# A gated cross-attention and mixture-of-experts block on one core: first tokens loaded by row tile, the first batch's work shared between engines, instruction lists written anew

## The chip, the core and the metric

The kernel runs on one core of a Trainium2 chip. The core has a matrix engine (TensorE, PE in the rows; its weight loads are PEld), VectorE (DVE), ScalarE (ACT), GpSimd (POOL), and SyncE (SP), which here only issues DMAs. Each engine runs its own list of instructions strictly in order and waits on semaphores; nothing is reordered while the kernel runs. The metric is the device time of one execution, in microseconds (us).

## What is computed

```python
# x (4,512,512); fside = weights (4,512,512); ctx = weights (4,512,256)
def smooth_quant_linear(x, w):            # x [T,D], w [O,D]
    s  = sqrt(max(amax(|x|,0),EPS) / max(amax(|w|,0),EPS))
    xs, ws = x / s, w * s
    x_scale = max(amax(|xs|,-1),EPS)/127;  w_scale = max(amax(|ws|,-1),EPS)/127
    return round(xs/x_scale) @ round(ws/w_scale).T * x_scale * w_scale.T
def layer1(x, guw, dw):                   # for each of the 4 batches
    gate, up = split(smooth_quant_linear(x, guw))
    return smooth_quant_linear(silu(gate) * up, dw)
def layer2(t):                            # 2048 tokens, width 512
    top-2 of 16 experts by softmax(t @ gate_w.T); each expert takes its first 256 tokens
    expert(t) = (silu(t @ w_gate) * (t @ w_up)) @ w_down        # inner width 352
    shared(t) = (silu(t @ ws_gate) * (t @ ws_up)) @ ws_down     # inner width 704
x = x + tanh(g_xattn) * layer1(layernorm(x), fside, ctx)
x = x + tanh(g_ffn)   * layer2(layernorm(x))
```

All of it is in float32. The matmuls of layer 2 split each operand into a rounded high part and the rest and add three products (high*high, high*low, low*high); they are the helper `three`, lines 1854 to 1856.

## The kernel before

Tokens lie as 4 batches of 512, each batch as 4 row tiles j of 128 partitions; x2 holds them throughout. A batch's layer 1 is a long chain that crosses all engines ("a" is its first product, "b" its second). The steps of a batch, by their names in the code:

- `stats_a` (DVE: bn_stats and bn_aggr of the four tiles), `norm_a` (POOL: a power gives 1/sqrt), `normalise_a` (ACT, L635: writes xn).
- The column peaks. For batch 0: `turn_w`, `turn_x` (PE transposes of weights w1 and of xn) and `amax_w`, `amax_x` (DVE, L1102). For later batches: `abs_w`, `abs_x` (ACT), `peaks_*` (DVE, L1107) and a short transpose.
- `ratio_a`, `root_a` (POOL), `smooth_a`; `row_rs`, `row_s` (PE) spread the factors over partitions; `scale_x`, `x_steps` (DVE), `copy_s` (ACT), `scale_w` (POOL, L486), `w_steps` (DVE, L1222).
- `quant_x`, `quant_w` (ACT, L642: rounding by adding a large constant), `turn_qx`, `turn_qw` (PE), `ints_x`, `ints_w` (ACT), `product_a` (PE, L1969), `dequant_a` (DVE, L1285), `silu_a` (ACT, L713), `gate_up` (DVE, L1299).
- The same for "b" with weights w2, ending in `add_x` (DVE, L1315), `stats_b`, `norm_b`, `normalise_b` (ACT, L754: writes y), `turn_y`, `x_hi` (ACT), `x_lo` (DVE), `logits` and the top-two choice. `store_x2n` writes y to DRAM. `positions`, `slot_rows`, `table`, `add_table`, `index` turn the choices of all four batches into the token list of each expert.

Beside it, POOL and ACT split the shared expert's weights: `split_gu_hi` (ACT), `split_gu_lo` (POOL, L502, four pieces), `split_d_*`. The first `shared_up` waits for all four pieces. The shared expert (`shared_up`, `shared_down` by batch, half and 128-wide chunk) fills PE between the steps of batches 1 to 3. Where nothing can fill, `keep_busy(n)` (L1896) writes n matmuls to an unused bank. Five of the eight token halves are done so; the three of `TAIL` are left for the end, where their shared expert runs as two more "experts" of inner width 352, while the routed rows are gathered back.

After that come the 16 experts. A step of expert e: `up` (its 352 inner columns as two chunks of 128 and a chunk of 96, whose gate and up parts are packed into one bank), `hidden` (ACT silu, L992; DVE product, L1715; ACT high part, L996; DVE low part, L1717), `down` with the sum over chunks, and `turn_tokens` for e+1. ACT's `weights_gu` (L793 to L796) and `weights_d` (L802) make the high parts of the next expert's weights, DVE's (L1446, L1459) the low parts. For a chunk m of the last unit ACT must also copy the packed up part (L990, L991) and DVE adds it (L1712).

What sets the order: for PE, DVE, ACT and POOL a list of calls written out by hand, up to the loop over experts; for SP the order of the `dma_start` calls. Expert 0's gate and up weights are loaded by themselves; expert 1's four transfers (gate 704 KB, up 704 KB, down 512 and 192 KB) go out together when `sh_gu` says that the last shared_up is done, and ACT's first `weights_gu(1, 0, 1)`, which stands ahead of `hidden(0, ...)` on ACT, waits for all four.

At the end DVE adds the gathered rows into x2 (`add_rows` by half batch, `add_last` by tile of batch 3, L1789 and L1792), and `last_rows` (L1783) adds the last unit's result, after which SP stores the tile.

## Time and profile before

| | us |
|---|---|
| median of 3 runs (579.65, 580.83, 579.65) | 579.65 |
| the profiled execution | 581.87 |
| its span, first to last instruction | 579.8 |
| PE busy in the span | 546.2 (94%) |
| DVE, ACT, POOL busy | 419.4, 331.0, 154.3 |
| mean granted clock of TensorE | 0.985 |

```profile
PE   7897879999999999999799999999999999999995
...
DVE  3778988998899786586376666766676776566766
...
PEclk9988999999999999999899999999999999999998
DMA  7930130014001130115757776666777767457742
```

These are busy tenths in 40 slices of 14.5 us. PE's line says nothing of use: the fillers of `keep_busy` count as busy. They all lie in the first 92 us. The granted clock falls in slices 3 and 4, in slice 20 (275 to 290 us) and in the last.

### The profile page before, as it was taken

Reading aid. Unit: us, or ns where it says so; the run is one execution under the profiler, and the core shown is the slowest. Engines: PE = TensorE matmul, PEld = TensorE weight load, DVE = VectorE, ACT = ScalarE, POOL = GpSimd, SP = SyncE. Lnnn points to the kernel's source line nnn. Section 1 sums busy time; section 2 is a strip of 40 time slices with the busy share of each in tenths; the row PEclk is TensorE's granted clock in tenths of the full one; section 3 lists DMA queues with packets and bytes.
Section 4 is the critical chain, followed back from the end, with each engine's and each line's share of the span. In section 5 each row is a group of like instructions: output and inputs, shape, how many; then the busy total and the mean of one; then the engine's idle time right before and its main releaser. Section 6 shows DMA issues by size and latency. Waiting matters only on the chain.

```text
span 579.8 us, 10175 instructions
## 1 busy us (share of the span) xinstructions
PE 546.2 (94%) x3768; PEld 464.0 (80%) x3776; DVE 419.4 (72%) x828; ACT 331.0 (57%) x570; POOL 154.3 (27%) x187
## 2 busy tenths in 40 slices
PE   7897879999999999999799999999999999999995
PEld 3453548986888788887799999999999999999983
DVE  3778988998899786586376666766676776566766
ACT  3285876686558527522367677766666666742321
POOL 3437780431043010104022211111111100166610
PEclk9988999999999999999899999999999999999998
DMA  7930130014001130115757776666777767457742
GB/s 265 386 131 2 37 136 11 2 37 145 1 5 35 73 101 1 77 46 165 244 165 263 246 252 222 222 222 227 242 244 260 245 218 241 148 167 214 232 147 99
DMA packets 45891, 89.52 MB, mean 154 GB/s; under 512 B 4304, under 2 KB 24784, under 8 KB 44832
## 3 DMA queue, kind: packets, MB, share of 16 engines
q1 hardware_dynamic: 40736, 72.26, 36.7%
q0 software_dynamic: 5120, 16.78, 9.3%
q8 instruction: 23, 0.38, 0.3%
q14 instruction: 12, 0.10, 0.0%
HBM read 72.25 MB, written 16.78 MB: 154 GB/s over the span
## 4 chain that ended last, share of the span: by engine, by line
PE 62%; DVE 19%; ACT 6%; POOL 6%; issue 4%; DMA 2%; another core or an unknown queue 1%; SPq 0%; DVEq 0%; POOLq 0%; ACTq 0%
PE ps_gu L1854 10%; PE ps_gu L1855 10%; PE ps_gu L1856 10%; PE ps_d L1854 6%; PE ps_d L1856 5%; PE ps_d L1855 5%; PE ps_a L2108 3%; PE ps_gu L1896 2%; POOL w L486 2%; DMA raw_d<-in_L_ffn_w_down 2%; PE ps_gu L2415 2%; POOL sw_lo L502 1%; PE ps_d L1875 1%; DVE bn_b L1093 1%; ACT y L754 1%
## 5 line engine op out<-in xcount | busy, mean ns | idle before, releaser
L1854 PE MATMUL ps_gu<-ex_xhi,w_hi 128*128 128x256 f32 x352 | 99.4, 283 | 0.2 <-DVE ex_xlo L1469 0.2
L1855 PE MATMUL ps_gu<-ex_xlo,w_hi 128*128 128x256 f32 x352 | 99.5, 283 | 0.0
L1856 PE MATMUL ps_gu<-ex_xhi,w_lo 128*128 128x256 f32 x352 | 99.4, 282 | 0.0
L1854 PEld LDWEIGHTS ps_gu<-ex_xhi,w_hi 128*128 128x128 f32 x352 | 67.0, 190 | 2.5 <-DVE ex_xlo L1469 0.5
L1855 PEld LDWEIGHTS ps_gu<-ex_xlo,w_hi 128*128 128x128 f32 x352 | 67.1, 191 | 1.8
L1856 PEld LDWEIGHTS ps_gu<-ex_xhi,w_lo 128*128 128x128 f32 x352 | 67.1, 191 | 0.0
L1854 PE MATMUL ps_gu<-xt_hi,sw_hi 128*128 128x256 f32 x220 | 65.1, 296 | 0.1
L996 ACT ACTIVATE ex_hhi<-ex_hid 128x256 fp32r<-128x256 f32 (+1 forms) x66 | 27.5, 417 | 64.6 <-DVE ex_hid L1715 58.0
L1855 PE MATMUL ps_gu<-xt_lo,sw_hi 128*128 128x256 f32 x220 | 62.0, 282 | 0.0
L1856 PE MATMUL ps_gu<-xt_hi,sw_lo 128*128 128x256 f32 x220 | 62.0, 282 | 0.0
L1854 PE MATMUL ps_d<-wd_hi,ex_hhi 128*128 128x512 f32 x132 | 54.3, 411 | 6.6 <-DVE ex_hlo L1717 6.5
L1717 DVE TENSOR_TENSOR ex_hlo<-ex_hid,ex_hhi 128x256 fp32r<-128x256 f32 (+1 forms) x66 | 28.0, 424 | 33.8 <-ACT ex_hhi L996 30.9
L1856 PE MATMUL ps_d<-wd_hi,ex_hlo 128*128 128x512 f32 x132 | 52.1, 395 | 0.0
L1855 PE MATMUL ps_d<-wd_lo,ex_hhi 128*128 128x512 f32 x132 | 51.9, 393 | 0.0
L586 POOL DMA_INDIRECT got<-expert_out_scratch,slot_col x32 | 33.1, 1036 | 67.4 <-DMA expert_out_scratch<-eo 51.6
L549 POOL COPY idx_col<-idx 128x2 uint32 (+1 forms) x16 | 5.5, 342 | 157.5 <-PE ps_a L2108 132.7
L1896 PE MATMUL ps_gu<-ident_b 128*128 128x512 bf16 x158 | 43.5, 414 | 3.6 <-POOL fold L446 3.6
L1854 PEld LDWEIGHTS ps_gu<-xt_hi,sw_hi 128*128 128x128 f32 x220 | 41.7, 190 | 3.2 <-issue 0.7
L1446 DVE TENSOR_TENSOR w_lo<-raw_gu,w_hi 128x1024 fp32r<-128x1024 f32 x36 | 43.8, 1218 | 0.0
L1855 PEld LDWEIGHTS ps_gu<-xt_lo,sw_hi 128*128 128x128 f32 x220 | 41.8, 190 | 1.0
L1856 PEld LDWEIGHTS ps_gu<-xt_hi,sw_lo 128*128 128x128 f32 x220 | 41.8, 190 | 0.0
L1715 DVE TENSOR_TENSOR ex_hid<-ex_silu,ps_gu 128x256 f32<-128x256 f32 x44 | 18.3, 416 | 32.2 <-ACT ex_silu L992 31.6
(255 smaller groups left out, 1411.4 us busy)
## 6 DMA issues: line engine op xcount, KB each, us to landing
raw_gu<-in_L_ffn_w_gate SPq DMA_DIRECT2D x16, 704.0 KB
raw_gu<-in_L_ffn_w_up SPq DMA_DIRECT2D x16, 704.0 KB
raw_d<-in_L_ffn_w_down SPq DMA_DIRECT2D x16, 512.0 KB
expert_out_scratch<-eo SPq DMA_DIRECT2D x16, 512.0 KB
w<-in_fside_BxS2xS SPq DMA_DIRECT2D x4, 1024.0 KB, 5.4
x2n_scratch<-y SPq DMA_DIRECT2D x4, 1024.0 KB, 3.9
x<-in_x SPq DMA_DIRECT2D x1, 3072.0 KB, 16.5
raw_d<-in_L_ffn_w_down SPq DMA_DIRECT2D x16, 192.0 KB
```

The source lines that it names most:

```text
L486: last = pool.tensor_tensor(w1[:, j, :], w1[:, j, :], line_a[:], ALU.mult)
L586: pool.indirect_dma_start(got[k][:, j, n, :], None, eo_dram, bass.IndirectOffsetOnAxis(slot_col[:, b, j, n:n + 1], 0)).then_inc(got_in[b][ ...
L996: act.activation(ex_hhi[0:k, m, :], ex_hid[0:k, (q + m) % 2, :], ACT.Copy).then_inc(ex_hi, 1)
L1446: dve.tensor_tensor(w_lo[q][:, g], raw_gu[q][:, g, :, 0:OWN], w_hi[q][:, g].bitcast(F32), ALU.subtract)
L1715: dve.tensor_tensor(ex_hid[0:k, (q + m) % 2, :], ex_silu[0:k, (q + m) % 2, :], up, ALU.mult).then_inc(ex_h, 1)
L1717: dve.tensor_tensor(ex_hlo[0:k, m, :], ex_hid[0:k, (q + m) % 2, :], ex_hhi[0:k, m, :].bitcast(F32), ALU.subtract).then_inc(ex_lo, 1)
L1854: pe.matmul(dst, a_hi, b_hi, start=start, stop=False)
L1855: pe.matmul(dst, a_hi, b_lo, start=False, stop=False)
L1856: return pe.matmul(dst, a_lo, b_hi, start=False, stop=stop)
L1896: pe.matmul(ps_gu[:, 1, :], ident_b[:], ident_b[:].unsqueeze(1).broadcast_to((P, J, P)), start=True, stop=True)
L2108: last = pe.transpose(ps_xt[:, c, h * P:(h + 1) * P], xg[q][:, h, c * P:(c + 1) * P], ident[:])
L2415: last = pe.matmul(folded, wb[q][:, c, :], ex_xhi[xq][:, c, :], start=(c == 0), stop=(c == C - 1))
```

## The change

Computed values stay the same. It has seven parts:

1. SP loads batch 0's tokens in four DMAs, one for each row tile, ahead of w1; `stats_a(0)` waits for each tile by itself.
2. For batch 0, `normalise_a` moves from ACT to DVE (between the second and third `amax_w`), half of `quant_w` moves to DVE (`quant_w_rest`), and `silu_a` and `gate_up` run as two halves. `normalise_b(0)` moves from ACT to DVE.
3. The lists of PE, ACT, DVE and POOL are written anew, from the first instruction to the first expert. The first `keep_busy` goes from 23 to 13. `stats_a(3)` moves from batch 0's `stats_b` to behind batch 1's. On DVE `w_steps(1)` goes ahead of `dequant_b(0, ...)`. On POOL `split_gu_lo(2)` goes behind the first `norm_b`.
4. Expert 1's down weights are loaded after its gate and up weights have landed, and `weights_gu(1)` waits for these alone.
5. `store_x2n(2)` goes behind the load of expert 0's gate and up weights; DVE's `weights_d(0, 0)` goes behind `tokens(0, 0)`.
6. In the very last unit the packed chunk is computed second instead of third (`part_at`).
7. At the end DVE's `add_last` steps all stand ahead of the last `hidden`, and `last_rows` adds the first half as soon as its own matmuls are done.

(The last two new functions in it, `normalise_a` and `quant_w_rest`, are DVE's; `normalise_b` on DVE is like the former, from x2 to y.)

```diff
+    def part_at(e, m):
+        return (0, 2, 1)[m] if e == NE - 1 else m
...
-            sp.dma_start(x2[:, 0], x_v[0]).then_inc(x0_in, 16)
+            for j in range(J):
+                sp.dma_start(x2[:, 0, j, :], x_v[0][:, j, :]).then_inc(x0_in[j], 16)
...
-            store_x2n(2)
             sp.wait_ge(gated_done, B)
             load_gu(0, wg_v[0], wu_v[0])
+            store_x2n(2)
             store_x2n(3)
...
-            load_raw(1, 1)
+            load_gu(1, wg_v[1], wu_v[1])
+            sp.wait_ge(raw_in[1], 32)
+            load_d(1, w_down[1])
...
+            def quant_w_first(a):
+                act.wait_ge(w_steps_done[LA], a + 1)
+                for j in range(HALF):
+                    last = act.activation(w1[:, j, :], w1[:, j, :], ACT.Copy, bias=MAGIC + LOW16, scale=small[LA]["w_inv"][:, j:j + 1])
+                last.then_inc(qw_done[LA], 1)
...
+            def silu_half(a, h):
+                t = slice(HALF * h, HALF * h + HALF)
+                for j in range(HALF * h, HALF * h + HALF):
+                    emptied_a(act, unit_a(a, A_H + j))
+                act.activation(gated[:, t, :], xn[:, t, 0:I2], ACT.Silu).then_inc(silu_done if h else silu_first_done, 1)
...
-                act.wait_ge(raw_in[q], 32 if isinstance(e, int) and e == 0 else 64 * k + 64)
+                act.wait_ge(raw_in[q], 32 if isinstance(e, int) and e < 2 else 64 * k + 64)
...
+            def normalise_a(a):
+                dve.wait_ge(rstd_a_done, 4 * a + 4)
+                for j in range(J):
+                    last = dve.tensor_scalar(xn[:, j, :], x2[:, a, j, :], rstd_a[:, a, j:j + 1], shift_a[:, a, j:j + 1], ALU.mult, ALU.add)
+                last.then_inc(xn_done, 1)
+            def quant_w_rest(a):
+                dve.wait_ge(w_steps_done[LA], a + 1)
+                for j in range(HALF, J):
+                    last = dve.tensor_scalar(w1[:, j, :], w1[:, j, :], small[LA]["w_inv"][:, j:j + 1], MAGIC + LOW16, ALU.mult, ALU.add)
+                last.then_inc(qw_rest_done, 1)
...
-                dve.wait_ge(ex_d, M * NE)
                 dve.wait_ge(sum_last, HALF)
                 for k in range(HALF):
                     j = HALF * h + k
+                    if k == 0:
+                        dve.wait_ge(first_half_done, 1)
+                    else:
+                        dve.wait_ge(ex_d, M * NE)
...
-            keep_busy(23)
+            keep_busy(13)
             turn_w(0, 0)
...
             turn_w(0, 3)
-            turn_w2(0, 0)
+            keep_busy(5)
             turn_x(0, 0)
...
-            hidden(E + 5, 1, 1)
-            add_last(1)
+            add_last(3)
             hidden(E + 5, 1, 2)
-            add_last(2)
-            add_last(3)
             last_rows()
```

The order on VectorE at the start: bn_a is the statistics, amax_w_a and amax_x_a the column peaks of weights and tokens, xn the normalised tokens. Before:

```order
L1084 BN_AGGR mv_a<-bn_a 128x2 x4
L1102 TENSOR_REDUCE amax_w_a<-ps_a 128x1 x4
L1102 TENSOR_REDUCE amax_x_a<-ps_a 128x1 x4
L1176 SCALAR_TENSOR_TENSOR recip_w_a<-amax_w_a,ones 128x4
L1183 RECIPROCAL recip_w_a<-recip_w_a 128x4
```

Now:

```order
L1110 BN_AGGR mv_a<-bn_a 128x2 x4
L1128 TENSOR_REDUCE amax_w_a<-ps_a 128x1 x2
L1326 TENSOR_SCALAR xn<-x_49,rstd_a,shift_a 128x512 x4
L1128 TENSOR_REDUCE amax_w_a<-ps_a 128x1 x2
L1128 TENSOR_REDUCE amax_x_a<-ps_a 128x1 x4
L1202 SCALAR_TENSOR_TENSOR recip_w_a<-amax_w_a,ones 128x4
```

Four passes over 512 elements have moved in among the eight reductions.

VectorE between batch 1's quantisation and the end of batch 0's layer 1: w_max_a is `w_steps(1)`, y<-ps_d is `dequant_b(0)`, x_49<-x_49,y is `add_x(0)`, bn_b and bn_a are `stats_b(0)` and `stats_a(3)`. Before:

```order
L1230 RECIPROCAL x_inv_a<-x_step_a 128x4
L1285 SCALAR_TENSOR_TENSOR y<-ps_d,x_step_b,line_b 128x512 x4
L1222 TENSOR_REDUCE w_max_a<-w_118 128x4
L1176 SCALAR_TENSOR_TENSOR w_step_a<-w_max_a,consts 128x4
L1230 RECIPROCAL w_inv_a<-w_step_a 128x4
L1315 TENSOR_TENSOR x_49<-x_49,y 128x2048
L1061 MEMSET consts 128x1
L1093 BN_STATS bn_b<-x_49 128x6 x4
L1061 MEMSET consts 128x1
L1097 BN_AGGR mv_b<-bn_b 128x2 x4
L1061 MEMSET consts 128x1
L1079 BN_STATS bn_a<-x_49 128x6 x4
```

Now:

```order
L1256 RECIPROCAL x_inv_a<-x_step_a 128x4
L1248 TENSOR_REDUCE w_max_a<-w_118 128x4
L1202 SCALAR_TENSOR_TENSOR w_step_a<-w_max_a,consts 128x4
L1256 RECIPROCAL w_inv_a<-w_step_a 128x4
L1311 SCALAR_TENSOR_TENSOR y<-ps_d,x_step_b,line_b 128x512 x4
L1370 TENSOR_TENSOR x_49<-x_49,y 128x2048
L1085 MEMSET consts 128x1
L1119 BN_STATS bn_b<-x_49 128x6 x4
L1085 MEMSET consts 128x1
L1123 BN_AGGR mv_b<-bn_b 128x2 x4
L1311 SCALAR_TENSOR_TENSOR xn<-ps_a,x_step_a,line_a 128x512
```

`w_steps(1)` has moved ahead of `dequant_b(0)`, and `stats_a(3)` is gone from here.

VectorE at the very end: got is a gathered row tile, the last row is `last_rows`. Before:

```order
L1712 TENSOR_TENSOR ex_up<-ex_up,ps_gu 64x256
L1715 TENSOR_TENSOR ex_hid<-ex_silu,ex_up 96x256
L1717 TENSOR_TENSOR ex_hlo<-ex_hid,ex_hhi 96x256
L1789 SCALAR_TENSOR_TENSOR x_49<-got_179,wts,x_49 128x512
L1792 SCALAR_TENSOR_TENSOR x_49<-got_179,wts,x_49 128x512
L1789 SCALAR_TENSOR_TENSOR x_49<-got_179,wts,x_49 128x512
L1792 SCALAR_TENSOR_TENSOR x_49<-got_179,wts,x_49 128x512
L1783 SCALAR_TENSOR_TENSOR x_49<-ps_d,tg,x_49 128x512 x2
```

Now:

```order
L1772 TENSOR_TENSOR ex_up<-ex_up,ps_gu 64x256
L1775 TENSOR_TENSOR ex_hid<-ex_silu,ex_up 96x256
L1777 TENSOR_TENSOR ex_hlo<-ex_hid,ex_hhi 96x256
L1852 SCALAR_TENSOR_TENSOR x_49<-got_179,wts,x_49 128x512
L1855 SCALAR_TENSOR_TENSOR x_49<-got_179,wts,x_49 128x512
L1775 TENSOR_TENSOR ex_hid<-ex_silu,ps_gu 128x256
L1777 TENSOR_TENSOR ex_hlo<-ex_hid,ex_hhi 128x256
L1846 SCALAR_TENSOR_TENSOR x_49<-ps_d,tg,x_49 128x512 x2
```

The last chunk is a plain one, and no gathered row stands between its low part and the last two additions.

## Rows read from the trace of the kernel before

**Rows 1.** the stages of the span (columns in the first line)
```profile
core 0: us, PE busy (x) PEld busy (x) DVE busy (x) ACT busy (x) POOL busy (x), PEclk, DMA share, GB/s
0.00:92.20 92.20, 75.85 (x423) 42.54 (x427) 67.77 (x126) 56.06 (x73) 50.30 (x71) 0.94 0.42 152
92.20:272.00 179.80, 174.91 (x1303) 149.84 (x1307) 149.21 (x359) 101.02 (x182) 36.02 (x41) 1.00 0.14 48
272.00:300.00 28.00, 24.08 (x156) 21.53 (x154) 14.18 (x26) 13.81 (x24) 5.10 (x6) 0.94 0.65 207
300.00:540.00 240.00, 239.89 (x1682) 221.80 (x1681) 162.19 (x276) 150.82 (x271) 53.70 (x61) 1.00 0.70 229
...
556.75:579.80 23.05, 15.83 (x98) 13.67 (x98) 16.41 (x28) 4.23 (x11) 0.00 (x0) 0.92 0.24 92
```

**Rows 2.** the page's costliest groups: filler matmuls, and the halving of the hidden values
```profile
L1896 PE MATMUL ps_gu<-ident_b 128*128 128x512 bf16 x158 | 43.5, 414 | 3.6 <-POOL fold L446 3.6
...
L1717 DVE TENSOR_TENSOR ex_hlo<-ex_hid,ex_hhi 128x256 fp32r<-128x256 f32 (+1 forms) x66 | 28.0, 424 | 33.8 <-ACT ex_hhi L996 30.9
```

**Rows 3.** timeline of the first 19 us (start us, us, engine line op)
```profile
3.62 8.03 PE L1896 MATMUL ps_gu<-ident_b 128*128 128x512 bf16 x23 [3.62 <-POOL fold L446]
...
10.51 2.93 ACT L635 ACTIVATE xn<-x,shift_a,rstd_a 128x512 f32<-128x512 f32 x4 [3.57 <-POOL shift_a L456]
...
12.12 1.34 DVE L1102 TENSOR_REDUCE amax_w_a<-ps_a 128x1 f32<-128x512 f32 x2 [3.62 <-PE ps_a L1875]
...
18.13 0.16 DVE L1176 SCALAR_TENSOR_TENSOR recip_w_a<-amax_w_a,ones 128x4 f32<-128x4 f32 x1
```

**Rows 4.** the issue of the first batch's weights at 1.25 (KB, us to landing)
```profile
w<-in_fside_BxS2xS SPq DMA_DIRECT2D x1, 1024.0 KB, 7.7
```

**Rows 5.** timeline, 30 to 46 us
```profile
30.95 2.56 ACT L642 ACTIVATE w<-w,w_inv_a 128x512 f32<-128x512 f32 x4
...
42.67 1.06 ACT L713 ACTIVATE gated<-xn 128x1024 f32<-128x1024 f32 x1 [0.40 <-DVE xn L1285]
...
45.01 5.04 POOL L502 TENSOR_TENSOR sw_lo<-raw_sgu,sw_hi 128x352 fp32r<-128x352 f32 x4
...
45.04 0.66 PE L1875 MATMUL ps_d<-ident,gated 128*128 128x128 f32 x4 [0.69 <-DVE gated L1299]
```

**Rows 6.** timeline, 65 to 86 us
```profile
65.41 4.99 POOL L486 TENSOR_TENSOR w<-w,line_a 128x512 f32<-128x512 f32 x4 [3.12 <-ACT line_a L677]
...
73.13 3.11 DVE L1315 TENSOR_TENSOR x<-x,y 128x2048 f32<-128x2048 f32 x1
...
81.13 2.93 ACT L754 ACTIVATE y<-x,shift_b,rstd_b 128x512 f32<-128x512 f32 x4 [1.84 <-POOL shift_b L456]
...
82.28 3.60 POOL L502 TENSOR_TENSOR sw_lo<-raw_sgu,sw_hi 128x352 fp32r<-128x352 f32 x4
```

**Rows 7.** groups of VectorE by line and shape (busy us, mean ns)
```profile
L1390 DVE TENSOR_SCALAR pos_oh<-slot_no,r_pos 128x256 bf16<-128x256 bf16 x32 | 6.6, 281 | 0.1
...
L1107 DVE TENSOR_TENSOR abs_b<-abs_b 128x512 f32<-128x512 f32 x6 | 4.1, 679 | 0.0
```

**Rows 8.** timeline around the first expert, 268 to 295 us
```profile
268.74 0.37 SPq L325 DMA_DIRECT2D raw_gu<-in_L_ffn_w_gate  x1
...
279.97 1.91 ACT L793 ACTIVATE w_hi<-raw_gu 128x2048 fp32r<-128x2048 f32 x1 [6.57 <-DMA raw_d<-in_L_ffn_w_down]
...
284.48 0.50 PE L1854 MATMUL ps_d<-wd_hi,ex_hhi 128*128 128x512 f32 x1 [3.70 <-DVE ex_hlo L1717]
...
294.89 1.90 ACT L793 ACTIVATE w_hi<-raw_gu 128x2048 fp32r<-128x2048 f32 x1
```

**Rows 9.** timeline of the end
```profile
572.43 0.74 DVE L1789 SCALAR_TENSOR_TENSOR x<-got,wts,x 128x512 f32<-128x512 f32 x1
...
572.56 0.50 PE L1854 MATMUL ps_d<-wd_hi,ex_hhi 96*128 96x512 f32 x1 [1.65 <-DVE ex_hlo L1717]
...
575.51 1.41 DVE L1783 SCALAR_TENSOR_TENSOR x<-ps_d,tg,x 128x512 f32<-128x512 f32 x2
```

More of the change, by code:

```diff
@@ L980, in _, with hidden @@
             shared_hi(2, 1, 5)
+            weights_d(0, 0)
             tokens(0, 0)
-            def hidden(e, q, m, first):
-                n, k = M * e + m, ROWS[m]
+            def hidden(e, q, m, first, part=None):
+                part = m if part is None else part
+                n, k = M * e + m, ROWS[part]
                 if first and m == 0:
@@ L1473, in _ @@
             amax_w(0, 1)
+            normalise_a(0)
             amax_w(0, 2)
@@ L1509, in _ @@
             x_steps(1)
+            w_steps(1)
             dequant_b(0, 0)
@@ L1513, in _ @@
             dequant_b(0, 3)
-            w_steps(1)
             add_x(0)
             stats_b(0)
-            stats_a(3)
             dequant_a(1, 0)
+            normalise_b(0)
             dequant_a(1, 1)
@@ L1670, in _ @@
             shared_lo(1, 1, 3)
+            count(2)
             shared_lo(1, 1, 4)
@@ L2426, in fill_d @@
                                  wd_hi[q][0:k, m, :], wd_lo[q][0:k, m, :], first, final)
+                    if halves is not None and h == 0:
+                        last.then_inc(halves, 1)
                 last.then_inc(ex_d, 1)
```

515 lines of the change are left out of this document (270 added, 245 removed).

## The prediction, as put down before the changed kernel had run

> **What bounds the kernel now.** I read the span by stages first [rows 1]. From 92.2 to 272 us, where the shared expert fills PE, PE is busy 174.91 of 179.8 us, and from 300 to 540, in the expert loop, 239.89 of 240. There only less matmul work would help, and the change takes none away. So the gain must come from three other places. Up to 92.2 us PE is busy 75.85 us, but 43.5 us of the filler matmuls [rows 2] all lie there: the useful part is about 32 us, and the stage is a chain through DVE (67.77 us busy), ACT and POOL. From 272 to 300 PE has 24.08 of 28 us. After 556.75 it has 15.83 of 23.05. The timeline of each place then shows which wait ends last.
>
> **The start, to the first batch's gated values.** PE runs 23 fillers up to 11.65 (8.03 us, 0.35 each), turns the weights, and DVE's eight reductions begin at 12.12 and end before 18.13 [rows 3]. The weights, issued at 1.25, are there 7.7 us later, at 8.95 [rows 4]: PE comes to them 2.7 us late. With 13 fillers it is there at 3.62 + 13 x 0.35 = 8.2, so the weights decide. They are issued some 1.4 us later now, behind four token DMAs instead of one, but behind the same bytes: 9.0 to 10.3, I take 9.4. Reductions then start at 9.4 + 0.47 = 9.9, 2.2 us earlier. Against this DVE has four new passes of 128x512 between them. No row shows such a pass: the nearest are a TENSOR_SCALAR over 256 bf16 elements with 0.28 us and a float32 pass over 512 elements with 0.68 [rows 7]. Each is off in one respect, so I take the middle, 0.45: 1.8 us (1.1 to 2.7). The gap between reductions pays 0.3 back. Net 2.2 - 1.8 + 0.3 = **0.7 us** earlier (-1.1 to 1.8). The row-tile load itself earns nothing here: ACT began `normalise_a` at 10.51 [rows 3] because POOL was done then, and DVE in the new list gets there at about 11.3.
>
> The Trainium skill, page "VectorE: DVE Perf Modes", section on the perf-mode tiers, has 1227 ns for a float32 tensor_scalar of 2048 elements in SBUF, some 0.3 to 0.4 us for a quarter as an estimate; with it this step would earn about 1.1 instead of 0.7.
>
> `quant_w(0)` takes ACT 2.56 us [rows 5], with ACT as the engine that all wait for; half of it on DVE beside ACT saves **1.3**. Silu takes 1.06 us after the last dequantisation [rows 5], and the product 1.2 behind it; in halves the first silu runs under the last two dequantisations and the second under the first product: **1.1**. Tokens' peaks start 3.1 us earlier, at 41.9 in place of 45.04 [rows 5].
>
> **From there to the first shared_up.** Batch 1's `scale_w` is five us of POOL, 65.41 to 70.4, and `w_steps(1)` waits for it; `add_x(0)` stands behind and begins at 73.13 [rows 6]. In the new list `scale_g` stands behind batch 1's `ratio_a`, so POOL takes the root, and ACT copies the factors, while DVE has work. Walking DVE's list with the durations of before, I get `w_steps(1)` at about 62 and the end of `stats_b(0)` at about 74.6 in place of 79.1: 1.4 more. `normalise_b(0)` takes ACT 2.93 us [rows 6]; on DVE 1.8 by the price above: 1.1 more. `stats_a(3)` (some 2.8 us, four passes of 0.68 and small ones) no longer delays `dequant_a(1)`, which the turn of y waits for on PE: 0.5. Together 3.1 + 1.4 + 1.1 + 0.5 = **6.1 us** at the first shared_up: 86.1 in place of 92.2. POOL must have split all four pieces by then: `norm_b(0)` ends at 76.5, then 1.3 + 3.6 + 3.6 [rows 6] gives 85.0. It just fits.
>
> One thing speaks against it. A split of the same size took 3.60 us at one place and 5.04 at another, beside DVE's work [rows 5, 6], and `add_x(0)` took 3.11 beside POOL [rows 6]. The Trainium skill, "SBUF — State Buffer", section "Who interferes with whom", has a rule for this: DVE's tensor_scalar from SBUF to SBUF, in its two-port modes, excludes GpSimd, "Whoever issues first gets the shared pair for the whole instruction". Both moved normalisations and `quant_w_rest` are such instructions, and the trace of before has none beside POOL. If each split takes 5.04 in place of 3.60, POOL is done at 85.0 + 2.9 = 87.9, and this part earns 4.3 instead of 6.1.
>
> **92 to 272 us.** PE's own work is the same; its 4.9 us of idle time may change. DVE is 149.21 of 179.8 us busy and now owes `stats_a(3)`. I take **1 us back** (between 4 back and 1.5 more gained): PE's fillers give room, but batch 3's chain must keep pace.
>
> **Expert 0 and 1.** Expert 1's weights go out at 268.74; ACT starts on them at 279.97, behind the last of four transfers, and PE waits 3.70 us, to 284.48, for `hidden(0, 0)`, which stands behind them on ACT [rows 8]. Now ACT waits for 1408 of 2112 KB. Of the 11.2 us, some 2 pass before data flow; two thirds of the rest is 6.1: 276.8, **3.2 us** earlier (0 if the gathers beside it slow it as much). The wait shrinks to 0.5. The clock comes with it: 0.94 over 28 us [rows 1] means 3.4 us at 1.2 instead of 2.4 GHz, 1.7 us of lost work; without the long wait I count **1.4** of that. The new SP wait holds back the down weights and then expert 2's load: 279.96 becomes some 281.2. ACT needs these at 294.89 [rows 8] less 4.6, 290.3, and that load takes about 8 us: it fits with 1 us. Sum **4.6** (0.5 to 5.2).
>
> `weights_d(0, 0)` behind `tokens(0, 0)` on DVE, and `store_x2n(2)` behind a load, cost nothing: both end before what waits for them, the first under PE's 5.7 us of up. If that cover goes, each costs up to 2 us.
>
> **The end.** The last chunk's low part is ready at 572.5 and PE waits 1.65 us for it [rows 9]. A plain chunk needs no copies of the packed part (two) and no addition, 0.4 us each; what is left is four steps of 0.42 [rows 2]: ready at 571.3, **1.2 us** earlier. Then DVE adds two tiles, four passes from 572.43, and only then the last rows, 575.51 to 576.92 [rows 9]. PE's first half ends 1.2 us after its start, so now: 572.5, and two additions to 574.0. That is 2.9 us earlier in all; DVE's third gathered tile may end just behind the silu, so I take **2.6** (1.2 to 3.6).
>
> **The sum.** 6.1 - 1.0 + 4.6 + 2.6 = 12.3 us. The profiled execution goes from 581.87 to 569.6 and its span from 579.8 to 567.5; the median of the runs lies 2.2 us below the profiled one, and from 579.65 I get **567.4**.
>
> **The rivals.**
> - The front's gain is given back where DVE sets the pace. For: 83% busy, and waits of PE there of 1 us and less show batch chains just in time. Against: DVE has 30 us idle there. Left are 4.6 + 2.6: 572.4.
> - POOL's splits decide, by the exclusion above: 569.2.
> - The change does not do what it says: the gate and up weights share their time with the gathers and land hardly earlier, and PE waits at expert 0 as before: 12.3 - 4.1, 571.5.
> - Slower: the token list. `index()` needs batch 3's top two, and PE's `turn_tokens(0, 0)` needs the gathers behind `index()`. If batch 3 is late by the new DVE list, PE has no fill left and waits; each us late is a us of time, plus half of what runs at the low clock. It decides from the point where batch 3's chain is 7.2 us later than now, as all that experts and end earn is then gone; a delay of 10 gives 582.5. Against it: PE reaches that place without waiting today, and the new list keeps the same steps between the last `table` and `turn_tokens`.
>
> **Chances.** As forecast 0.50; DVE's pace 0.27; POOL 0.10; weights land late 0.07; slower by the token list 0.06. A measurement can tell about 0.2% (1.2 us) from no change. The first four are all faster by more, less 0.03 for the pace rival at its worst together with a bad end: faster 0.91, same 0.03, slower 0.06. The range takes in the bounds: best 7.5 + 1.5 + 5.2 + 3.6 = 17.8 gives 561.9, worst of the faster cases 3 - 4 + 3.5 + 1.7 = 4.2 gives 575.5. The tail beyond both is under 0.2.
>
> **What would show it.** The first shared_up at 86 us (a later start with PE fillers before it: the front failed; POOL's last sw_lo ending there: the port). The new TENSOR_SCALAR lines at 0.28 to 0.68 us each. PE's idle time from shared_up to `turn_tokens(0, 0)` under 7 us. ACT's first w_hi of expert 1 some 8 us after its load's issue, PE's longest wait there under 1 us and no slice with a low clock. PE's last wait under 0.6 us and the last x addition directly behind the last matmul. The forecast is wrong if the stage from 86 to 265 grows by more than its share, or if the weights' load is slowed by the gathers.

## The result, and the profile after

The changed kernel takes 583.31 us (median of 7 runs, 582.73 to 585.32) against 579.65 (578.91 to 580.83, 7 runs) for the one before: ratio 1.0067, 95% interval 1.0052 to 1.0082. It is slower, by 3.7 us in the median, where I had said 12 faster. Its profiled execution took 582.95 us, with a span of 580.9; PE is busy 540.6 us of it, DVE 431.6, ACT 325.2, POOL 152.0, at a mean clock of 0.985. The experiments ran later, on four chips (the kernel before beside each), where in many executions the end of every kernel is slower, the kernel before among them (579.3 to 597.3 us on the last of them), so that each ratio compares only those runs of a kernel that lie within 1.5% of its fastest. Besides the ratios I compare landmarks of the traces; those of "before" and "changed" come from the first measurement.

Four of them cut the span: the first shared_up on PE, POOL's copy of the first token list (`idx_col`), POOL's copy for the last expert, and POOL's first gather of result rows. From the third to the fourth it is 55.2 to 55.4 us in all traces. Of the changed kernel they read (timeline: start us, us, engine line op):

```profile
100.17 0.28 PE L1917 MATMUL ps_gu<-xt_hi,sw_hi 128*128 128x256 f32 x1
...
271.75 0.22 POOL L558 COPY idx_col<-idx 128x2 uint32<-128x2 uint32 x1 [25.55 <-DVE idx L1463]
...
454.13 0.31 POOL L558 COPY idx_col<-idx 128x2 uint32<-128x2 uint32 x1 [9.91 <-PE ps_a L2173]
...
509.46 0.97 POOL L595 DMA_INDIRECT got<-expert_out_scratch,slot_col  x1 [51.61 <-DMA expert_out_scratch<-eo]
```

The kernel before has 92.36, 262.83, 449.45 and 504.73 there, and ends at 579.8 instead of 580.9. The difference by stretch:

| stretch | before | changed | difference | predicted |
|---|---|---|---|---|
| start to first shared_up | 92.36 | 100.17 | +7.8 | -6.1 |
| to the first token list | 170.47 | 171.58 | +1.1 | +1.0 |
| to the last expert's tokens | 186.62 | 182.38 | -4.2 | -4.6 |
| to the first result rows | 55.28 | 55.33 | 0 | 0 |
| from there to the end | 75.07 | 71.44 | -3.6 | -2.6 |

Three of the four terms came out within a microsecond. The whole miss is in the first stretch, which alone is 13.9 us off. Its end in the windows of the changed kernel (columns in the first line), to be held against the first line of [rows 1]:

```profile
core 0: us, PE busy (x) PEld busy (x) DVE busy (x) ACT busy (x) POOL busy (x), PEclk, DMA share, GB/s
0.00:92.20 92.20, 63.35 (x369) 36.31 (x373) 72.54 (x118) 44.62 (x58) 46.85 (x71) 0.92 0.41 140
...
272.00:300.00 28.00, 26.89 (x170) 22.88 (x170) 18.84 (x32) 13.56 (x25) 10.07 (x11) 1.00 0.72 231
...
55.00:60.00 5.00, 3.04 (x14) 2.28 (x13) 4.83 (x10) 0.76 (x2) 4.49 (x6) 0.78 0.01 2
60.00:65.00 5.00, 4.84 (x35) 3.65 (x34) 4.90 (x5) 4.27 (x10) 2.76 (x4) 0.88 0.01 2
70.00:75.00 5.00, 3.72 (x16) 1.95 (x17) 3.97 (x7) 4.12 (x6) 5.00 (x5) 0.66 0.00 0
...
80.00:85.00 5.00, 2.37 (x11) 0.70 (x8) 3.79 (x7) 2.82 (x3) 4.38 (x7) 1.00 0.45 171
85.00:90.00 5.00, 0.00 (x0) 0.00 (x0) 5.00 (x2) 0.00 (x0) 5.00 (x7) 0.51 0.00 0
90.00:95.00 5.00, 3.05 (x12) 2.18 (x13) 3.91 (x6) 1.19 (x2) 0.70 (x1) 0.50 0.47 193
```

From 85 to 90 us PE and ACT do nothing at all, DVE has two instructions and POOL seven; and when PE resumes, it is at half its clock until about 95. Its clock is also low from 55 to 65 and from 70 to 75 us, which will matter below. The timeline of the changed kernel has the instruction that all wait for:

```profile
82.19 1.26 POOL L522 TENSOR_TENSOR sd_lo<-raw_sd,sd_hi 64x512 fp32r<-64x512 f32 x1
...
82.28 9.62 DVE L1333 TENSOR_SCALAR y<-x,rstd_b,shift_b 128x512 f32<-128x512 f32 x4 [0.95 <-POOL shift_b L465]
...
83.42 7.28 POOL L511 TENSOR_TENSOR sw_lo<-raw_sgu,sw_hi 128x352 fp32r<-128x352 f32 x8
...
91.95 1.12 PE L1938 MATMUL ps_d<-ident,y 128*128 128x128 f32 x4 [9.54 <-DVE y L1333]
```

That is `normalise_b(0)`: four passes priced at 1.8 us that took 9.62. The answer for that line alone shows how they share it, one long and three short:

```profile
L1333 DVE TENSOR_SCALAR y<-x,rstd_b,shift_b x4: 534/840/7644, 82.3 to 91.4; 128x512 f32<-128x512 f32 x4
```

The nanoseconds are shortest, median and longest. The long one is the first, from 82.28 to 89.92; POOL's row of splits, one behind the other, ends at 90.70, and the last of them starts at 89.6. POOL's eight took 0.91 us each in the mean, as long as before ([rows 6]: four in 3.60).

The start lost a little too. The statistics begin sooner than the single load allowed, but the fourth tile comes late, and so do the weights:

```profile
4.44 0.69 DVE L1105 BATCH_NORM_STATS2 bn_a<-x 128x6 f32<-128x512 f32 x1 [2.00 <-DMA x<-in_x]
...
7.78 0.69 DVE L1105 BATCH_NORM_STATS2 bn_a<-x 128x6 f32<-128x512 f32 x1 [1.00 <-DMA x<-in_x]
...
10.46 0.66 PE L1938 MATMUL ps_a<-ident,w 128*128 128x128 f32 x4 [2.42 <-DMA w<-in_fside_BxS2xS]
...
12.42 1.91 DVE L1326 TENSOR_SCALAR xn<-x,rstd_a,shift_a 128x512 f32<-128x512 f32 x4
...
18.73 0.17 DVE L1202 SCALAR_TENSOR_TENSOR recip_w_a<-amax_w_a,ones 128x4 f32<-128x4 f32 x1
...
40.08 4.05 POOL L511 TENSOR_TENSOR sw_lo<-raw_sgu,sw_hi 128x352 fp32r<-128x352 f32 x4 [2.92 <-ACT sw_hi L627]
...
41.93 2.76 DVE L1347 TENSOR_TENSOR gated<-gated,xn 128x512 f32<-128x512 f32 x2
```

`recip_w_a`, the end of the eight reductions, stands at 18.73 against 18.13 [rows 3], and the two half products of gate and up take 2.76 us, beside a split of POOL. Experts and end did as foreseen; of the timeline and of SP's issues:

```profile
276.89 0.38 SPq L331 DMA_DIRECT2D raw_gu<-in_L_ffn_w_gate  x1
...
285.04 1.91 ACT L816 ACTIVATE w_hi<-raw_gu 128x2048 fp32r<-128x2048 f32 x1 [3.21 <-DMA raw_gu<-in_L_ffn_w_up]
...
575.40 0.50 PE L1917 MATMUL ps_d<-wd_hi,ex_hhi 128*128 128x512 f32 x1 [0.44 <-DVE ex_hlo L1777]
...
576.48 1.41 DVE L1846 SCALAR_TENSOR_TENSOR x<-ps_d,tg,x 128x512 f32<-128x512 f32 x2 [1.13 <-PE ps_d L1919]
```

ACT has its weights 8.15 us after their issue (11.2 before, [rows 8]), PE's longest wait there is 0.5 us instead of 3.70, and the last wait is 0.44 instead of 1.65 [rows 9].

### The profile page after: what moved, and what is told of

It reads as the page before. It is cut to its first block, busy times and chain, and to the rows that moved or that the text cites. A ratio compares the mean times of both kernels' runs of the same rounds, so it can differ in the third digit from the quotient of the medians.

```text
span 580.9 us, 10139 instructions
## 1 busy us (share of the span) xinstructions
PE 540.6 (93%) x3748; PEld 460.7 (79%) x3756; DVE 431.6 (74%) x839; ACT 325.2 (56%) x561; POOL 152.0 (26%) x187
## 4 chain that ended last, share of the span: by engine, by line
PE 63%; DVE 18%; ACT 4%; DMA 3%; issue 3%; POOL 1%; SPq 0%; DVEq 0%; ACTq 0%
PE ps_gu L1917 10%; PE ps_gu L1918 10%; PE ps_gu L1919 10%; PE ps_d L1917 6%; PE ps_d L1919 5%; PE ps_d L1918 5%; PE ps_a L2173 3%; DMA raw_d<-in_L_ffn_w_down 2%; DVE y L1333 2%; PE ps_a L2034 2%; PE ps_gu L2483 1%; PE ps_d L1938 1%; DMA raw_gu<-in_L_ffn_w_up 1%; PE ps_a L1953 1%; PE ps_gu L2485 1%
## 5 line engine op out<-in xcount | busy, mean ns | idle before, releaser
L1917 PE MATMUL ps_d<-wd_hi,ex_hhi 128*128 128x512 f32 (+1 forms) x132 | 54.4, 412 | 1.5 <-DVE ex_hlo L1777 1.2
L595 POOL DMA_INDIRECT got<-expert_out_scratch,slot_col x32 | 34.6, 1082 | 68.7 <-DMA expert_out_scratch<-eo 51.6
L1919 PE MATMUL ps_d<-wd_hi,ex_hlo 128*128 128x512 f32 (+1 forms) x132 | 52.1, 394 | 0.0
L1918 PE MATMUL ps_d<-wd_lo,ex_hhi 128*128 128x512 f32 (+1 forms) x132 | 51.9, 393 | 0.0
L1918 PEld LDWEIGHTS ps_gu<-xt_lo,sw_hi 128*128 128x128 f32 x220 | 41.9, 190 | 0.8
L1959 PE MATMUL ps_gu<-ident_b 128*128 128x512 bf16 x138 | 37.6, 400 | 3.6 <-POOL fold L455 3.6
L562 POOL DMA_INDIRECT xg<-x2n_scratch,idx_col x32 | 34.1, 1065 | 17.6 <-POOL idx_col L558 12.7
```

The lines of the kernel that those rows point to most:

```text
L562: pool.indirect_dma_start(xg[q][:, h, :], None, x2n_dram, bass.IndirectOffsetOnAxis(idx_col[:, q, h:h + 1], 0)).then_inc(xg_in[q], 16)
L595: pool.indirect_dma_start(got[k][:, j, n, :], None, eo_dram, bass.IndirectOffsetOnAxis(slot_col[:, b, j, n:n + 1], 0)).then_inc(got_in[b][ ...
L1917: pe.matmul(dst, a_hi, b_hi, start=start, stop=False)
L1918: pe.matmul(dst, a_hi, b_lo, start=False, stop=False)
L1919: return pe.matmul(dst, a_lo, b_hi, start=False, stop=stop)
L1959: pe.matmul(ps_gu[:, 1, :], ident_b[:], ident_b[:].unsqueeze(1).broadcast_to((P, J, P)), start=True, stop=True)
```

## The experiments

The landmarks of the traces in us, with the stretches behind them. Names are those of the runs below.

| kernel | first shared_up | to token list | to last expert | result rows to end |
|---|---|---|---|---|
| before | 92.36 | 170.5 | 186.6 | 75.1 |
| changed | 100.17 | 171.6 | 182.4 | 71.4 |
| e1, e8: changed, normalise_b(0) on ACT | 92.28, 94.30 | 172.6, 172.7 | 181.8, 182.4 | 81.3, 85.2 |
| e2: changed, POOL waits | 92.25 | 172.1 | 182.3 | 89.9 |
| e3: before, normalise_b(0) on DVE | 95.96 | 170.6 | 187.4 | 83.6 |
| e4: before, down weights last | 89.56 | 170.6 | 182.6 | 83.5 |
| e5: before, new end | 91.61 | 170.6 | 188.2 | 73.0 |
| e7, e12: before, both | 91.58, 90.37 | 170.6, 170.6 | 182.7, 182.6 | 71.3, 72.0 |
| e6: e1 and one load | 91.92 | 172.8 | 182.2 | 79.6 |
| e9: changed, other form | 100.72 | 171.6 | 182.2 | 89.8 |
| e10: e6, held split, fillers | 88.75 | 172.8 | 182.9 | 82.1 |
| e11: e7, one gather ahead | 90.28 | 170.6 | 182.5 | 102.2 |
| e13: changed again | 101.63 | 171.6 | 182.4 | 84.4 |
| e14, e15, e16: e10, ACT's stream shifted | 89.84, 89.08, 89.65 | 172.8, 172.8, 172.8 | 183.2, 182.7, 181.9 | 89.7, 83.6, 84.2 |

My theory after the result: DVE's passes over SBUF stand still as long as POOL's instructions follow each other without a gap. The rivals: the form of pass is slow by itself, or the front is late for other reasons and the pass only fills a wait.

**Put the step back, or clear the way for it.** e1 takes `normalise_b(0)` out of DVE's list and puts it into ACT's:

```diff
@@ ACT's list
             split_gu_hi(3)
+            normalise_b(0)
             x_hi(0, 0)
@@ DVE's list
             dequant_a(1, 0)
-            normalise_b(0)
```

> The changed kernel with one step put back: normalise_b(0) runs on ACT again, behind its last split, instead of on DVE. Theory A (DVE's pass is starved by GpSimd's splits of the shared weights): ACT writes y in about 2.9 us from 82.3 on, so y is there at 85.2 instead of 91.9; GpSimd's four pieces end near 90.7 as now and set the first shared_up at about 92.5 instead of 100.7. Time 575.5 us (573 to 577.5), from 583.3. Rival B (the front is late for other reasons, the new list above all, and the pass only fills a wait): first shared_up stays at 99 or later, time 582 to 583.5.

e2 leaves it on DVE and makes POOL wait for it:

```diff
             norm_b(0)
+            pool.wait_ge(x2n_done, 1)
             split_d_lo(1)
```

> The changed kernel with one wait more: GpSimd starts its last three splits (the small down piece and gate-up pieces 2 and 3) only when normalise_b(0) on DVE is done. Theory A (starvation by GpSimd): each of DVE's four passes of 128x512 takes 0.45 to 0.6 us, y is there at 84.3; GpSimd's 8.6 us of splits then end near 93, the first shared_up is at about 93.5, time 576 us (574 to 579). Rival B (this form of pass is slow by itself, whoever is beside it): the passes still take 9.6 us in sum, GpSimd ends at 100.5, time 583 to 585.

In both the first shared_up moved to where the theory had it or sooner: 92.28 (92.5 expected) and 92.25 (93.5). Not all of the 7.9 us against the changed kernel's 100.17 is the pass, though. `shift_b`, from which y can start, already stands at 82.04 in the changed kernel and at 80.03 and 81.06 in these two; PE's clock was low between 55 and 75 us in the changed kernel's trace (0.78, 0.88, 0.66), and 1.00 there in both of these. From the start of `shift_b` to the first shared_up the changed kernel takes 18.1 us (18.1 again in e13), e1 12.3 and e2 11.2: the pass and the low clock behind it cost 5.9 to 6.9 us. The 2.0 us before it, against e1, are PE's slow steps: it spreads `rsmooth_a` in 2.04 us from 57.74 where e1 takes 1.16, and all that waits for it is late. In e2's timeline the same four passes at the same place take 1.91 us, with POOL idle behind them:

```profile
81.29 1.91 DVE L1334 TENSOR_SCALAR y<-x,rstd_b,shift_b 128x512 f32<-128x512 f32 x4 [0.58 <-POOL shift_b L465]
...
83.28 1.27 POOL L522 TENSOR_TENSOR sd_lo<-raw_sd,sd_hi 64x512 fp32r<-64x512 f32 x1 [2.03 <-DVE y L1334]
...
84.52 7.63 POOL L511 TENSOR_TENSOR sw_lo<-raw_sgu,sw_hi 128x352 fp32r<-128x352 f32 x8
...
87.98 3.39 DVE L1134 TENSOR_TENSOR abs_b<-abs_b 128x512 f32<-128x512 f32 x1
```

So form and data are not slow, POOL's row of splits is what the passes wait for. The last line shows it on another form: a pass that takes 0.68 us elsewhere [rows 7] took 3.39, until POOL was nearly through. Times: e1 has ratio 1.0124 (1.0057 to 1.0190), e2 1.0089 (1.0029 to 1.0149). The 575.5 and 576 us that I expected were not seen, though the first result rows are gathered at 502.07 and 501.92, earlier than in the kernel before (504.73): both traces lose it after that, in 81.3 and 89.9 us instead of 71.4. e8 is e1 once more:

> The same kernel as in the first of these experiments (normalise_b(0) back on ACT, all else as changed), since there the part after 505 us was disturbed. Up to the first gather of result rows it stood at 502.07 us, where the kernel before stood at 504.73 and the changed one at 509.46. Theory (starvation was the whole loss of the front, and the rest of the front is neutral): 575.5 us, ratio 0.993, 1.3% under the changed kernel. Rival (something else of the new lists costs time later): 579 or more.

It gave 580.81 us at best and a ratio of 1.0069 (1.0018 to 1.0120); its trace stands at 504.68 at the first result rows and then takes 85.2 us. By time the rival came out (579 or more): the loss comes in the last stretch, whose cause is taken up below.

**One part alone in the kernel before.** e3:

```diff
@@ ACT's list
-            normalise_b(0)
@@ DVE's list
             dequant_a(1, 0)
+            normalise_b(0)
             dequant_a(1, 1)
```

> The kernel before with one part of the change alone: normalise_b(0) on DVE, behind dequant_a(1, 0), and not on ACT. Theory A (starvation): GpSimd's splits run there too, from about 81 to 89, so y is complete only near 89 instead of 84, the first shared_up moves from 92.4 to about 97, time 583 to 588 us against 579.65. Rival B (the prediction's price, 0.45 us a pass): y 1.1 us earlier, time 578.5 to 579.7.

```profile
82.99 3.76 POOL L502 TENSOR_TENSOR sw_lo<-raw_sgu,sw_hi 128x352 fp32r<-128x352 f32 x4
...
83.25 4.70 DVE L1299 TENSOR_SCALAR y<-x,rstd_b,shift_b 128x512 f32<-128x512 f32 x4
...
88.00 1.12 PE L1882 MATMUL ps_d<-ident,y 128*128 128x128 f32 x4 [3.58 <-DVE y L1299]
```

Here POOL has only four splits in a row, and the passes take 4.70 us. y is there at 88.0 (I said 89), the first shared_up at 95.96 (97), ratio 1.0123 (1.0075 to 1.0172). The wait follows the length of POOL's row: 3.5 us of it are left when DVE begins, and 2.8 us are lost over e2's 1.91; in the changed kernel 8.4 are left and 7.7 lost. In the old lists `split_gu_lo(2)` was done long before; the new lists put it directly behind `split_d_lo(1)`, so the row is twice as long.

**Another form of the same step.** e9:

```diff
-                    last = dve.tensor_scalar(y[:, j, :], x2[:, b, j, :], rstd_b[:, j:j + 1], shift_b[:, j:j + 1], ALU.mult, ALU.add)
+                    last = dve.scalar_tensor_tensor(out=y[:, j, :], in0=x2[:, b, j, :], scalar=rstd_b[:, j:j + 1],
+                                                    in1=shift_b[:, j:j + 1].broadcast_to((P, D)), op0=ALU.mult, op1=ALU.add)
```

> The changed kernel with normalise_b(0) still on DVE, at the same place in its list, but as four scalar_tensor_tensor instructions (in1 is the shift, one value per row, spread over the row) instead of four tensor_scalar. The trace of the changed kernel has scalar_tensor_tensor passes beside GpSimd's work at 0.70 to 0.75 us each. Theory (only some forms of a DVE instruction are kept waiting by GpSimd, tensor_scalar among them): four passes in 2.8 to 3.2 us, y at 85.3 in place of 91.9, first shared_up at 92 to 93 in place of 100.2. Rival (any DVE pass from SBUF to SBUF waits while GpSimd's instructions follow each other): 8 us or more again, first shared_up at 100.

```profile
81.55 10.64 DVE L1333 SCALAR_TENSOR_TENSOR y<-x,rstd_b,shift_b 128x512 f32<-128x512 f32 x4
...
82.55 7.10 POOL L511 TENSOR_TENSOR sw_lo<-raw_sgu,sw_hi 128x352 fp32r<-128x352 f32 x8
```

My theory of forms fell, the rival is right: 10.64 us, the first pass alone 8.65, first shared_up at 100.72, ratio 1.0286 (1.0183 to 1.0388). The scalar_tensor_tensor passes that run undisturbed beside POOL, the dequantisations, read their product from PSUM. So the name of the instruction does not decide, and where its inputs lie seems to. Nor is every read of SBUF held up: the kernel before computes the statistics of x, in SBUF, from 76.28 to 78.75 us beside POOL's down splits (74.04 to 78.62) in 0.69 and 1.86 us (one pass, then three), as long as in the changed kernel with POOL idle. Which property of a pass decides, no run here isolates.

**The load by row tile.** e6 is e1 with one DMA for the first tokens, and the waits on it to match:

```diff
-            for j in range(J):
-                sp.dma_start(x2[:, 0, j, :], x_v[0][:, j, :]).then_inc(x0_in[j], 16)
+            sp.dma_start(x2[:, 0], x_v[0]).then_inc(x0_in, 16)
...
```

> As the one before, and the first tokens loaded by one DMA again instead of four by row tile. Theory (four issues ahead of the weights and a late fourth tile delay statistics and the first transposes): the first statistics end near 8.1 us instead of 8.5 to 9.7, PE's first transposes start near 9.5 instead of 10.5 to 11.5, and the time falls by 1 to 1.5 us against that kernel, to 574.3. Rival (the pieces cost nothing): the same time within 0.3 us.

The first statistics end at 8.2, PE turns the weights from 9.00 (10.46 in the changed kernel and 10.47 in e1), and `recip_w_a` stands at 17.26 instead of 18.73: 1.5 us for four issues ahead of the weights. The weights are issued at 2.65 us behind four issues and at 1.25 behind one, and land 7.8 and 7.7 us later: the later issue counts in full. In the six traces with four loads `recip_w_a` stands at 18.73 to 20.21, in the five of the same lists with one load (e6, e10, e14 to e16) at 16.91 to 17.57. The gain lives as far as `shift_b` (78.55 instead of e1's 80.03), but the first shared_up is only 0.4 earlier, at 91.92: PE waits 3.3 us for y, and its granted clock is 0.65 and 0.67 from 80 to 90 us. The time was 575.77 us at best and 587.28 in the median of six runs, which gives no ratio with an interval; the expected 574.3 was not reached.

**Both repairs of the rest.** e10 is e6 with two edits more: it holds POOL's first split until the gated values are done, and gives PE eight fillers ahead of the first transpose of y:

```diff
@@ POOL's list
             norm_a(1)
+            pool.wait_ge(gated_done, 1)
             split_gu_lo(0)
@@ PE's list
+            keep_busy(8)
             turn_y(0, 0)
```

> The kernel with normalise_b(0) on ACT and one load of the first tokens, and two edits more: GpSimd starts its first split only when the first batch's gated values are done, and PE has eight fillers more ahead of turn_y(0, 0). Theory for the first edit (the two half products of gate and up, 2.76 us, waited for that split): they take 1.3 us, and the first transposes of the gated values start at 41.8 instead of 43.3. Theory for the second (PE idle before turn_y lets the clock fall): no 5 us slice under 1.00 from 80 to 92, and from shift_b to the first shared_up 10.0 to 11.2 us instead of 13.4. First shared_up at 87.5 to 90 instead of 91.9. Rival: the half products are slow by their form or size, 2.7 us again, and the clock falls whatever PE does there, 91 to 92.

```profile
40.11 0.68 DVE L1346 TENSOR_TENSOR gated<-gated,xn 128x512 f32<-128x512 f32 x1
40.95 0.69 DVE L1346 TENSOR_TENSOR gated<-gated,xn 128x512 f32<-128x512 f32 x1 [0.16 <-ACT gated L736]
...
41.70 0.66 PE L1936 MATMUL ps_d<-ident,gated 128*128 128x128 f32 x4 [0.57 <-DVE gated L1346]
...
80.00:85.00 5.00, 3.46 (x23) 2.05 (x21) 1.68 (x3) 3.31 (x6) 5.00 (x7) 1.00 0.45 184
85.00:90.00 5.00, 4.62 (x29) 2.89 (x27) 4.83 (x7) 4.83 (x6) 1.55 (x2) 1.00 0.06 26
```

Both theories hold: the halves take 0.68 us each instead of 2.76 together, and the clock stays at 1.00. The first shared_up is at 88.75, the earliest of all. But the held split only moves the wait: it now runs beside `abs_a(1)`, whose two passes take 1.63 and 1.31 us instead of 1.22 and 0.69 (e6), and `shift_b` is only 0.55 us earlier than in e6. The other 2.6 us come behind it, where the clock is full (10.75 us from `shift_b` to the first shared_up instead of 13.37). Still the old lists reach the first shared_up at 89.56 to 91.61 when their clock does not fall from 85 to 90 us (e4, e5, e7, e11, e12), and the new lists then need 2.2 us more up to the token list: it comes at 261.5 to 262.7 in e10 and e14 to e16, and at 260.2 to 262.8 with the old lists (e3, the only one with the step on DVE, aside). So a repaired front is worth nothing over the old one; ratio of e10 1.0071 (1.0018 to 1.0124).

**The later parts alone.** e4 has only expert 1's loads and their waits, e5 only the new end (parts 6 and 7 of the change):

```diff
@@ e4
-            load_raw(1, 1)
+            load_gu(1, wg_v[1], wu_v[1])
+            sp.wait_ge(raw_in[1], 32)
+            load_d(1, w_down[1])
...
-                act.wait_ge(raw_in[q], 32 if isinstance(e, int) and e == 0 else 64 * k + 64)
+                act.wait_ge(raw_in[q], 32 if isinstance(e, int) and e < 2 else 64 * k + 64)
...
```

> The kernel before with one part of the change alone: expert 1's gate and up weights are loaded first, its down weights behind them, and ACT's and SP's waits as in the changed kernel. The prediction's term: ACT starts on the weights some 8 us after their issue instead of 11.2, PE's wait of 3.70 us at 284.48 shrinks to about 0.5 and the clock stays up: 4.6 us less, 575.0 us (574.4 to 577). Rival (the transfers share their time with the gathers, or expert 2's load is late in turn): PE waits on, 578.5 to 579.7.

> The kernel before with the end of the change alone: in the last unit the packed chunk comes second, the last additions are split by half, and DVE's additions of gathered rows stand earlier in its list. The prediction's term is 2.6 us (1.2 to 3.6): 577.0 us from 579.65, ratio 0.9955. The two traces in hand say a little more: from the first gather of result rows to the end the kernel before takes 75.1 us and the changed one 71.4, so 576.0 (ratio 0.9937) is possible. Rival (the last wait only moves to the output's stores): 579 to 580.

e4 needs 182.6 us from token list to last expert instead of 186.6, ratio 0.9907 (0.9847 to 0.9967): the term of 4.6 stands with 4.0 (5.6 beside e5, whose 188.2 is the longest). e5 has a ratio of 0.9979 (0.9926 to 1.0032), which decides nothing; in its trace the end takes 2.0 us less than before, with an idle stretch of ACT in it. e7 has both, and e12 is e7 again:

> The kernel before with the two later parts of the change together, expert 1's down weights last and the end, and none of the first 92 us. If the two terms add (4.6 and 2.6, or 3.9 and 3.6 by the traces in hand): 572.3 us, ratio 0.987 (0.984 to 0.990), and it beats both kernels. Rival (they share their gain, since both raise the clock or both wait for the same transfer): 575 to 576.

> The kernel before with expert 1's down weights last and the new end, once more, beside the one before on the same chip. If the two parts add it stands at 571.5 to 573.5 us in its undisturbed runs, 6 to 7.5 us under the kernel before, ratio 0.987 to 0.990; rival: the first time was luck, 576 or more.

Their traces have spans of 571.5 and 570.8 us, 8.3 and 9.0 under the kernel before, the shortest of the study. The ratios are 0.9857 (0.9771 to 0.9944) and 0.9969 (0.9906 to 1.0031); the best times 572.90 and 572.85 beside 578.68 and 579.18. These ratios rest on few runs, three of six and four of twelve. So the kernel before with these two parts is the one that I would keep: in the first of the two it beats the kernel before beyond its interval, in the second that is not shown, and beside the changed kernel it was never run.

**The end on other chips.** e11 sets one constant in e7, how many tiles of result rows are gathered ahead:

```diff
-    AHEAD = 2
+    AHEAD = 1
```

> The kernel before with expert 1's down weights last and the new end, and with result rows gathered one tile ahead instead of two. It asks for the cause of ACT's idle stretches of 2.6 to 11 us between 510 and 555 us that the traces put to nothing inside the core, and that come and go from run to run. Theory (the load of ACT's next block of instructions, a DMA of 16 KB, waits behind GpSimd's gathers): fewer packets in flight let it through, the stretches are gone or under 3 us, and the spread of the times (572.9 to 585.3 with two ahead) falls to 3 us, around 573 to 576. Rival (gathers have nothing to do with it): the spread stays 10 us or more; with the gathers too slow, all times lie above 576.

It takes 609.3 us (ratio 1.0448, 1.0379 to 1.0518), six of seven runs within 1.8 us: the gathers themselves now set the pace, the last is issued at 588 us. There is no idle stretch of the disputed kind in its trace, but with everything slower that does not decide. e13 is the changed kernel unaltered, the control, and e14 to e16 shift ACT's stream without changing its work:

```diff
@@ ACT's list of e10; 64, 128, 192
+            for _ in range(64):
+                act.sem_inc(padded, 1)
             copy_s(0)
```

> The changed kernel as it is, beside the one before, on whichever chip this turns out to be: the control for the experiments whose end (after 505 us) was disturbed. Theory A (those chips or hours disturb the end of every kernel, and the new lists suffer more): the changed kernel lies at 583 to 595 us with ACT stretches of 2.6 to 11 us without work between 510 and 555, ratio 1.01 or more. Theory B (only the kernels with normalise_b(0) moved suffer): it stays at 582.7 to 585.3, ratio 1.007.

> The kernel with the held split and the added fillers (581.8 us of span, 583.8 us at its best in ten runs), with 64 increments of an unused semaphore at the start of ACT's list, where ACT waits for data anyway. All work is the same; only the place of each later instruction in ACT's stream moves. Theory (ACT stops at the border of a block of its instructions whose load came late behind the gathers): the border moves out of or within the stretch of gathers, the stops of ACT change place, and the span changes by several us, to 571 to 575 if the border leaves the stretch. Rival (the stops come from the data or the gathers themselves): same places, same 581 to 584.

> As the one before, with 128 increments. Theory: stops in other places again, at best none and 573 to 576 us. Rival: as without them, 583 to 587.

> As the one before, with 192 increments. Theory: stops in other places again, at best none and 573 to 576 us. Rival: as without them, 583 to 587.

The changed kernel took 594.35 to 602.18 us there (583 to 595 expected), ratio 1.0214 (1.0108 to 1.0320): its own end suffers too (84.4 us instead of 71.4), so theory A holds and e1, e2 and e8 were not special. Theory A also says that the new lists suffer more, and that stays unexplained: with the new lists ten of eleven traces need 79.6 us or more from the result rows to the end, the old lists with the old or the new end 71.3 to 75.1 in four of six (e11 aside).

The shifted kernels took 583.91 to 593.13, 584.71 to 589.60 and 583.73 to 593.16 us (ratios 1.0022, 1.0053 and 1.0101), e10 583.84 to 592.06. Each trace of them has a stop of 4.7 to 8.4 us. The time does not hang on the place in ACT's stream; that theory fell. They show one thing more. They ran beside e13 on the same chip and differ from it, shift aside, by the step back on ACT, the single load, the held split and the fillers; their medians are 585.21 to 586.50 us against 597.22, and their first shared_up comes 11.8 to 12.6 us sooner. So by time too, and not only by landmark, most of what the new front lost comes back with these repairs. The step alone was not run beside the changed kernel.

## Why the prediction was wrong, point by point

- **The step that failed** is "`normalise_b(0)` takes ACT 2.93 us; on DVE 1.8 by the price above: 1.1 more". The price of a pass was right: e2 measured 1.91 us for the four. What I left out was who runs beside it: in the changed kernel the four took 9.62 us. The rival of the port had the right pair of engines but the wrong loser: it slowed POOL's splits by 1.4 us each and kept DVE whole, and so gave 569.2. In the trace POOL lost nothing and DVE stood 7.7 us. With PE's clock at 0.50 behind that, it is 5.9 to 6.9 us at the first shared_up (18.1 us from `shift_b`, against 12.3 and 11.2 in e1 and e2). The prediction's own sum had the collision: it let the passes start at 76.5, and POOL's splits run from 76.5 to 85.0.
- **It is the largest term of the miss and not the only one.** The first shared_up was to stand at 86.1 and stood at 100.2, 14.1 us later. 5.7 of these were gone before the pass began (`norm_b(0)` was to end at 76.5 and ended at 82.2), by the points below. Even without the step, e1 reaches the first shared_up at 92.3 us, 6.2 behind the forecast and no sooner than the kernel before.
- The Trainium skill, page "SBUF — State Buffer", section "Who interferes with whom", from which that rival came, holds further than I took it. That the other engine blocks fully is what the 7644 ns show. It also says that a DVE instruction with two inputs in SBUF contends with a GpSimd instruction that reads SBUF; e9, the half products and `abs_b` in e2 agree, and I had priced the half products without it.
- **Start to recip_w_a, 0.7 us earlier**: it came 0.6 later. The weights were ready for PE at 10.46 where I took 9.4: issued 1.4 us later, as I had said, they also landed some 1.5 later (at 10.45 instead of 8.95), and I had taken two thirds of the 1.4 away because the bytes ahead were the same. e6 gives the size: with one load `recip_w_a` stands at 17.26, 1.5 us earlier. Even 17.26 is no sure gain: the old lists stand between 17.23 and 18.13 there (e4, before).
- **The halves of silu and product**: 1.3 + 1.1 us were to put the transposes of gated at 41.9. They stood at 44.74. e6 takes 1.5 of the difference away, e10 1.6 more, of which the halves beside no split are 1.2: 41.70, against 43.88 to 45.04 with the old lists. The half of `quant_w` has no experiment of its own.
- **The chain of batch 1, 1.4 us**: `w_steps(1)` was to start at 62 and started at 67.3, behind POOL's `scale_w(1)`. From the transposes of gated to `shift_b` the changed kernel needs 37.3 us, with the slow steps of PE in it; with full clock the new lists need 35.3 and 35.2 (e1, e2) and the old ones 35.7 (e4). So the gain is 0.5 us at most, and 2.0 were lost in that execution (2.1 in e13). A low clock elsewhere in this stretch cost e6 and e9 nothing (35.3 each). I had walked DVE's list and not ACT's and POOL's with the same care.
- **The comparison itself** flattered the change: the 92.36 of before holds a low clock (0.70 from 85 to 90 us). From `shift_b` to the first shared_up it needs 11.5 us, and the same lists at full clock 10.0 (e4, e5, e7, e12). So 1.5 us of that front are the clock's. Its first shared_up differs by 2.8 us between executions (89.56 in e4), the rest of it before `shift_b`.
- **92 to 272 us, 1 us back**: 1.1, with 4.9 us of idle time of PE up to `turn_tokens(0, 0)`, as before. In the kernels whose batch chain is on time it is 2.1 to 2.3, still inside the 4 that I allowed.
- **Expert 0 and 1, 4.6 us**: 4.2 in the traces, 4.0 by e4 alone. Landing 8.15 us after the issue (8.1 predicted), longest wait 0.5 (0.5), clock 1.00 over the 28 us (0.94 before; in e7 and e12, where this stage lies at the same time as before, 1.00 too).
- **The end, 2.6 us**: 3.6. Of it, 1.1 us are a wait of PE in the kernel before at 555 us, behind one of the ACT stops that the last section tells of; what is left is 2.5.
- **The rival of DVE's pace** did not happen, and the slower rival by the token list was not the way either: the list came 8.9 us late, but because the whole front was, and from the list to `turn_tokens(0, 0)` on PE it is 7.9 us as it was 8.5 before.

## What to carry to other kernels

Before a step moves to VectorE, look at what GpSimd has in its queue at that moment, not only at the step's own price: a pass over SBUF can wait for the whole row of GpSimd instructions that follow each other, so place it where GpSimd must wait for something, let GpSimd wait for it (one line, and some 6 to 7 us at the next landmark here), or leave the step on ScalarE. A hold can move the wait to the next pass, as e10's did, so look there too. And measure a change part by part: here two of its parts are worth 7 to 8 us together by the traces, and the rest gave all of it back.
